# The spread of B into PSUM: its bf16 parts and its selecting columns on 128 partitions instead of 48

## The chip, the cores and the metric

One core of one Trainium2 chip runs the whole program. The metric is the device time of one execution in microseconds. The launch has 3 timed runs of the kernel before.

## What is computed

An image of 128 x 128 tokens with 64 channels goes through two blocks, each a token mixer and a feed-forward part with a residual sum: row attention, a sigmoid recurrence, a selective state-space scan over the 16384 tokens in both directions, and a mixture of 8 experts. The change is in the scan, of which the reference says:

```
dA = jnp.exp(dt[..., None] * A)
dBx = dt[..., None] * Bm[:, :, None, :] * xc[..., None]
def step(h, inp):
    dA_t, dBx_t, C_t = inp
    h = dA_t * h + dBx_t
    y = jnp.einsum('bds,bs->bd', h, C_t)
    return (h, y)
...
y_fwd = _mamba(x_flat, *params)
y_bwd = jnp.flip(_mamba(jnp.flip(x_flat, axis=1), *params), axis=1)
```

There are 128 inner channels (d) and 16 states (s). B (`Bm`) and C hold one number for each token and state, the same for all channels.

## The kernel before

The program is a row of stages, and barriers separate them. The scan is the longest, from about 760 to 2530 us of the span. It works on chunks of 1024 tokens (`TC`), 16 forward (`forward`, chunks 0 to 15) and then 16 backward (`backward`, 16 to 31). In each chunk the channels lie on the 128 partitions and the tokens along the free axis, and the 16 states come one after another. All five engines run the same list of units (chunk n, state s), written out in program order by `run`; semaphores with counts hold them together. Nothing is scheduled by a tool.

For one state s of a chunk:

- ACT makes the decay exp(dt A_s), into an SBUF ring `s_dA` (`decay_v`, L1469) or, for some states, into PSUM (`decay_g`, L1474).
- The input dt B_s x is made in one of three ways. For the states in `BY_VECTOR` (8 of 16 forward, 10 of 16 backward) PE spreads row B_s over 128 partitions into the PSUM tile `s_pu` (`spread_b`, L1303), and DVE multiplies it there by `s_dtx` (L1611). For `BY_SCALAR` (4 forward, none backward) ACT scales transposed data and PE turns them into `s_pu` (L1294). The remaining states (4 forward, 6 backward) have B_s spread by a DMA into `s_bb`, and POOL multiplies (L1546).
- DVE scans: h = decay * h + input (L1635), with two tiles `s_pu` used in turn, so that PE may spread for state s only once the scan of state s-2 is done.
- POOL multiplies h by C_s, which a DMA has spread into `s_cc`, giving `s_hc` (`read_c`, L1553). PE adds it up over the states in `s_py` with an identity as weights (`total`, L1316). A ring of 4 tiles `s_hc` ties POOL to PE: POOL may write the tile of state s once PE has added that of state s-4.

The spread of B_s by PE works on three bf16 parts (high, middle, low) of B in f32. `part_high`, `part_rest` and so on make them one chunk ahead, SP stores them and loads them again as `bcs`, 48 rows = 3 parts x 16 states of 1024 tokens, one half of the tile for each parity of the chunk. The weights are one column of `sel` (48 x 16, ones at rows s, 16+s and 32+s), repeated 128 times, so that the sum of the three parts reaches every output partition. Each half of 512 tokens takes one matmul and one weight load; the whole program has 288 spreads and so 576 of each.

Between these, PE also does the convolution (L1249), the projections of the next chunk and, going backward, the output projection (`project`, L1345, 64-column matmuls).

At the head of the scan SP issues `load_n(0)`, `load_n(1)`, `load_flat(0)` (L1684), `store_parts(0)`, `load_parts(0)` and then the spreads by DMA. POOL sets `s_zero` (L1565) and then waits for its first work, `part_rest` (L1533). The functions that the diff touches are these:

Of the kernel before, what the change touches and what calls it, by code (L numbers as in the profile page):

```python
# [6 lines left out]
BF16 = mybir.dt.bfloat16  # L7
# [942 lines left out]
INNER, STATES, RANK, TAPS = 128, 16, 4, 4  # L950
TC = 1024
# [14 lines left out]
def state_space_stage(nc, c, W, y_scratch, rows, nd, split):  # L966

    with ExitStack() as ctx:
        def sb(name, shape, dt=F32):
# [4 lines left out]
            z=sb("ss_wz", [D, INNER]), bc=sb("ss_wbc", [INNER, BCW]), dt=sb("ss_wdt", [INNER, INNER]),  # L974
            out=sb("ss_wout", [INNER, D]), cb=sb("ss_cb", [INNER, 1]), db=sb("ss_db", [INNER, 1]),
            dd=sb("ss_D", [INNER, 1]), dg=sb("ss_dg", [INNER, INNER]), A=sb("ss_A", [INNER, STATES]),
            sel=sb("ss_sel", [3 * STATES, STATES], BF16))


        zero = sb("ss_zero", [D, PAD + 1])  # L980
# [141 lines left out]
def state_scan(nc, c, nd, k, y_scratch, rows, split):  # L1122
# [9 lines left out]
    with ExitStack() as ctx:  # L1132
# [4 lines left out]
            return c.sem("s_" + name)  # L1137
        ns = sb("n", [128, 2, TC + 2 * PAD])
        xc, dt, dtx = sb("xc", [128, 2, TC]), sb("dt", [128, 2, TC]), sb("dtx", [128, 2, TC])
        bcs = sb("bcs", [3 * STATES, 2, TC], BF16)  # L1140
        brow = sb("brow", [BCW, TC])
        flat, rest = sb("flat", [128, FLAT]), sb("rest", [128, FLAT])
        parts = sb("parts", [128, 3, FLAT], BF16)
# [75 lines left out]
        def _(pe):  # L1219
# [77 lines left out]
            def spread_b(w, n, par, s):  # L1297

                if s == w.v[0]:
                    pe.wait_ge(p_loaded[par], 8 * (n + 2 - par))  # L1300
                need(pe, scanned, n * U + s - 1)
                for hf in halves:
                    ins = nc.tensor.matmul(p_u[s % 2][:, hf],  # L1303
                                           lhsT=k["sel"][:, s:s + 1].to_broadcast([3 * STATES, 128]),
                                           rhs=bcs[:, par, hf], start=True, stop=True)
                ins.then_inc(b_made, 1)

# [213 lines left out]
        @block.gpsimd  # L1521
        def _(pool):
            def linear_and_log(w, m, par):

                pool.wait_ge(relu_made, m + 1)
                pool.wait_ge(log_made, m + 1)
                nc.gpsimd.tensor_tensor(tc[:, :], tc[:, :], tb[:, :], ALU.add).then_inc(sum_made, 1)

            def part_rest(w, m, par):
                pool.wait_ge(high, m + 1)  # L1530
                need(pool, lowest, m)
                need(pool, middle, m)
                nc.gpsimd.tensor_tensor(rest[:, :], flat[:, :], parts[:, 0, :], ALU.subtract).then_inc(remained, 1)  # L1533

            def part_low(w, m, par):
                pool.wait_ge(middle, m + 1)
                pool.wait_ge(remained, m + 1)
                nc.gpsimd.tensor_tensor(parts[:, 2, :], rest[:, :], parts[:, 1, :], ALU.subtract).then_inc(lowest, 1)

            def inject(w, n, par, s):  # L1540
                r = w.g.index(s)
                if r == 0:
                    pool.wait_ge(dtx_done, n + 1)
                pool.wait_ge(b_spread[r % B_RING], 16 * (w.upto(G, n, B_RING) + r // B_RING + 1))
                need(pool, scanned, w.past(G, n, s, lambda v: B_RING))
                nc.gpsimd.tensor_tensor(dbx[:, r % B_RING, :], dtx[:, par, :], bb[:, r % B_RING, :],  # L1546
                                        ALU.mult).then_inc(g_injected, 1)

            def read_c(n, s):
                pool.wait_ge(c_spread[s % C_RING], 16 * (n * (U // C_RING) + s // C_RING + 1))  # L1550
                pool.wait_ge(scanned, n * U + s + 1)
                need(pool, summed, n * U + s + 1 - RING)
                nc.gpsimd.tensor_tensor(hc[:, s % RING, :], h[:, s % RING, :], cc[:, s % C_RING, :],  # L1553
                                        ALU.mult).then_inc(read, 1)

            def unit(w, n, par, s, before, nxt):
                mw, m, mpar, ms = after(w, n, par, s + INJECT_AHEAD, nxt)
                if mw is not None and ms in mw.g:
                    inject(mw, m, mpar, ms)
                if s:  # L1560
                    read_c(n, s - 1)
                elif before is not None:
                    read_c(n - 1, U - 1)

            nc.gpsimd.memset(zero[:, :], 0.0).then_inc(zeroed, 1)  # L1565
            prepare = [(8, part_rest), (9, linear_and_log), (10, part_low)]
            assert min(forward.g) >= INJECT_AHEAD
            run(pool, unit, lambda w: prepare)
            read_c(ALL - 1, U - 1)
# [3 lines left out]
        def _(dve):  # L1573
# [64 lines left out]
                if mw is not None and ms in mw.v:  # L1638
                    inject(mw, m, mpar, ms)

            dve.wait_ge(zeroed, 1)
            prepare = [(9, lost), (10, step_sum), (12, dt_x)]
            tail = {forward: (), backward: [(LAG_SUM - 1, gate), (14, add_x)]}
            run(dve, unit, lambda w: prepare, tail.get)
# [4 lines left out]
        @block.sync  # L1649
        def _(sp):  # L1650
            way_of = lambda m: backward if m >= NC else forward

            def load_n(m):
                if m >= 2:
                    sp.wait_ge(conv, m - 1)
                need(sp, z_made, m - NC - 1)
                W_ = TC + 2 * PAD
                for half in range(2):
                    sp.dma_start(ns[half * D:(half + 1) * D, m % 2, :],
                                 nd[:, base(m) + 1 - half:base(m) + 1 - half + W_]).then_inc(n_loaded[m % 2], 16)  # L1660

            def spread_row(dst, m, row, spread):
                src = rows[m // NC][m % NC, row, :].rearrange("(a t) -> a t", a=1).to_broadcast([128, TC])
                sp.dma_start(dst, src).then_inc(spread, 16)

            def spread_c(n, s):
                if s == 0:
                    sp.wait_ge(r_stored, 16 * (n + 1))
                need(sp, read, n * U + s + 1 - C_RING)
                spread_row(cc[:, s % C_RING, :], n, STATES + s, c_spread[s % C_RING])  # L1670

            def spread_b(n, s):
                w = way_of(n)
                r = w.g.index(s)
                if r == 0:
                    sp.wait_ge(r_stored, 16 * (n + 1))
                need(sp, g_injected, w.upto(G, n) + r + 1 - B_RING)
                spread_row(bb[:, r % B_RING, :], n, s, b_spread[r % B_RING])

            def load_flat(m):  # L1680
                sp.wait_ge(r_stored, 16 * (m + 1))
                need(sp, remained, m)
                src = rows[m // NC][m % NC, 0:STATES, :].rearrange("r (b t) -> (r b) t", t=FLAT)
                sp.dma_start(flat[:, :], src).then_inc(f_loaded, 16)  # L1684

            def store_parts(m):
                sp.wait_ge(lowest, m + 1)
                sp.dma_start(split[m // NC][m % NC, :, :, :].rearrange("k s (b t) -> (s b) k t", t=FLAT),
                             parts[:, :, :]).then_inc(p_stored, 16)

            def load_parts(m):
                sp.wait_ge(p_stored, 16 * (m + 1))
                need(sp, b_made, way_of(m).upto(V, m - 1))
                sp.dma_start(bcs[:, m % 2, :],
                             split[m // NC][m % NC, :, :, :].rearrange("k s t -> (k s) t")).then_inc(p_loaded[m % 2], 16)

            def store_y(n):
                sp.wait_ge(y_taken, 2 * n + 2)
                sp.dma_start(y_scratch[:, base(n):base(n) + TC], yo[:, :]).then_inc(y_stored, 16)

            def load_y(n):
                if n == NC:
                    sp.wait_ge(y_stored, 16 * NC)
                need(sp, y_joined, n - NC)
                sp.dma_start(yf[:, :], y_scratch[:, base(n):base(n) + TC]).then_inc(y_loaded, 16)

            load_n(0)
            load_n(1)
            load_flat(0)
            store_parts(0)  # L1710
            load_parts(0)
            for s in range(4):
                if s in forward.g:
                    spread_b(0, s)
            for n in range(ALL):
                last = n == ALL - 1
                for s in range(U):
                    if s == 8 and 0 < n <= NC:
                        store_y(n - 1)
                    if n >= NC and s == (10 if n == NC else 3):  # L1720
                        load_y(n)
                    m, ms = n + (s + 4) // U, (s + 4) % U
                    if m < ALL and ms in way_of(m).g:
                        spread_b(m, ms)
                    spread_c(n, s)
                    if s == 8 and not last:
                        load_flat(n + 1)
                    if s == 13 and not last:
                        store_parts(n + 1)
                    if s == 14 and not last:  # L1730
                        load_parts(n + 1)
                    if s == 11 and n + 2 < ALL:
                        load_n(n + 2)
# [278 lines left out]
```

## Time and profile before

| | |
|---|---|
| median of 3 runs | 2724.7 us (2724.25 to 2729.43) |
| profiled execution, its own time | 2724.38 us |
| its span, first to last instruction | 2722.6 us |
| mean granted TensorE clock | 0.938 |
| PE, DVE, ACT, POOL busy | 2412.6, 2180.0, 1798.4, 1940.2 us |

The span is what the trace covers; the profiled execution's own time is 1.8 us longer. The granted clock is a share of full speed: 1.00 is 2.4 GHz and 0.50 is 1.2 GHz, and a value between them is a stretch that has both. Busy time of an engine counts the time in which its instructions ran. PE's weight loads are listed apart (PEld), since they overlap its matmuls.

### The profile page before, as it was taken

How to read it: one execution, taken by the hardware profiler on the slowest of the kernel's cores; microseconds unless marked ns; L12 is line 12 of the kernel's file. 1: busy time of each engine (PE TensorE's matmuls, PEld its weight loads, DVE VectorE, ACT ScalarE, POOL GpSimd, SP SyncE). 2: the span in 40 equal slices, each digit the busy share in tenths (PEclk: the TensorE clock that was granted, in tenths of full speed). 3: DMA queues.
4: the chain of work that ended last, by engine and by line, in shares of the span. 5: the costliest groups of instructions: out<-in, count | busy, mean ns of one | idle time of the engine just before them, and what ended most of it. 6: DMA issues, size and time to landing. Idle time of an engine off the chain costs nothing. (4 is left out here: it accounts for less than half of the span.)

```text
span 2722.6 us, 40183 instructions
## 1 busy us (share of the span) xinstructions
PE 2412.6 (89%) x10620; PEld 1195.4 (44%) x10620; DVE 2180.0 (80%) x2229; ACT 1798.4 (66%) x4094; POOL 1940.2 (71%) x1197
## 2 busy tenths in 40 slices
PE   6999999857459899999999999999999999998587
PEld 6577667624324334434433433333333333333533
DVE  4455555560639999999999999999999999998766
ACT  4688778743657778878877875665566556653376
POOL 3900000030239999999999999999999999999379
PEclk7799999969679999999999999999999999999799
DMA  3000000000146767676666767777777677775022
GB/s 66 11 10 10 10 8 9 7 1 0 43 130 222 220 227 228 223 230 220 229 228 221 234 226 250 243 237 235 238 247 238 225 235 246 239 223 189 3 62 62
DMA packets 186408, 421.08 MB, mean 155 GB/s; under 512 B 66548, under 2 KB 87513, under 8 KB 186330
## 3 DMA queue, kind: packets, MB, share of 16 engines
q1 hardware_dynamic: 184794, 416.01, 48.1%
q10 hardware_dynamic: 1536, 4.20, 0.5%
q8 instruction: 29, 0.48, 0.1%
q14 instruction: 49, 0.40, 0.0%
HBM read 387.63 MB, written 24.12 MB: 151 GB/s over the span
## 5 line engine op out<-in xcount | busy, mean ns | idle before, releaser
L1553 POOL TENSOR_TENSOR s_hc<-s_h,s_cc 128x1024 f32<-128x1024 f32 x512 | 1201.2, 2364 | 62.9 <-PE s_py L1316 44.5
L1316 PE MATMUL s_py<-s_hc,ident 128*128 128x512 f32 x2048 | 1019.0, 623 | 8.6 <-DVE s_yo L1598 8.6
L1635 DVE TENSOR_TENSOR_SCAN s_h<-s_dA,s_state,s_pu 128x1024 f32<-128x1024 f32 x330 | 770.4, 2342 | 29.5 <-PE s_pu L1294 6.1
L1316 PEld LDWEIGHTS s_py<-s_hc,ident 128*128 128x128 f32 x2048 | 365.1, 194 | 456.1 <-issue 419.3
L1469 ACT ACTIVATE s_dA<-s_dt,ss_A 128x1024 f32<-128x1024 f32 x352 | 401.7, 1142 | 9.1 <-ACT s_brow L1432 7.7
L1474 ACT ACTIVATE s_pu<-s_dt,ss_A 128x1024 f32<-128x1024 f32 x160 | 178.4, 1115 | 319.1 <-DVE s_h L1635 313.9
L1546 POOL TENSOR_TENSOR s_dbx<-s_dtx,s_bb 128x1024 f32<-128x1024 f32 x160 | 378.0, 2363 | 7.4 <-DMA s_bb<-rows_scratch 7.4
L1611 DVE TENSOR_TENSOR s_pu<-s_pu,s_dtx 128x1024 f32<-128x1024 f32 x288 | 349.7, 1214 | 24.5 <-PE s_pu L1303 24.5
L1635 DVE TENSOR_TENSOR_SCAN s_h<-s_pu,s_state,s_dbx 128x1024 f32<-128x1024 f32 x150 | 350.2, 2335 | 16.8 <-ACT s_pu L1474 16.6
L234 POOL MEMSET rn_n_add<- 128x1 f32 x1 | 0.1, 103 | 403.9 <-POOLq L78 403.9
L1303 PE MATMUL s_pu<-s_bcs,ss_sel 48*128 48x512 bf16 x576 | 175.2, 385 | 92.4 <-DVE s_h L1635 92.3
L628 ACT ACTIVATE ar_ex<-ar_sc,ar_mn 128x128 f32<-128x128 f32 x512 | 199.1, 390 | 44.3 <-DVE ar_mn L534 44.2
L530 DVE TENSOR_TENSOR ar_sc<-ar_pss,at_bias 128x512 f32<-128x512 f32 x128 | 88.5, 692 | 109.8 <-PE ar_pss L468 105.7
L1303 PEld LDWEIGHTS s_pu<-s_bcs,ss_sel 48*128 48x128 bf16 x576 | 33.6, 95 | 307.9 <-DVE s_h L1635 198.5
L1452 ACT ACTIVATE s_sT<-s_dtxT,s_bT 128x128 f32<-128x128 f32 x512 | 156.4, 388 | 0.2
L481 PE MATMUL ar_pst<-ident,ar_ex 128*128 128x128 f32 x1024 | 151.0, 292 | 0.7 <-ACT ar_exT L621 0.7
L1902 PE MATMUL ee_ps<-ex_we,ex_xg 128*128 128x512 f32 x256 | 112.7, 601 | 30.2 <-DMA ex_xg<-ex_xT 30.2
L481 PEld LDWEIGHTS ar_pst<-ident,ar_ex 128*128 128x128 f32 x1024 | 126.3, 194 | 16.3 <-ACT ar_ex L628 0.8
L1249 PE MATMUL s_pp<-s_n,ss_taps 128*128 128x512 f32 x256 | 124.4, 611 | 9.9 <-DMA s_n<-n_scratch 9.9
L544 DVE SCALAR_TENSOR_TENSOR ar_og<-ar_gate,ar_pso 128x128 f32<-128x128 f32 x128 | 36.8, 288 | 97.4 <-PE ar_pso L494 97.4
L1920 ACT ACTIVATE ee_hw<-ee_ps,ex_wt 128x64 f32<-128x64 f32 x384 | 91.9, 316 | 14.8 <-PE ee_ps L1902 5.1
L1481 ACT COPY s_state<-s_h 128x1 f32<-128x1 f32 x510 | 86.8, 179 | 18.5 <-DVE s_h L1635 17.9
(267 smaller groups left out, 3700.6 us busy)
## 6 DMA issues: line engine op xcount, KB each, us to landing
s_cc<-rows_scratch SPq DMA_DIRECT2D x512, 512.0 KB, 4.6
s_bb<-rows_scratch SPq DMA_DIRECT2D x160, 512.0 KB, 5.0
s_n<-n_scratch SPq DMA_DIRECT2D x64, 258.0 KB, 5.6
y_scratch<-s_yo SPq DMA_DIRECT2D x16, 512.0 KB, 5.4
s_yf<-y_scratch SPq DMA_DIRECT2D x16, 512.0 KB, 6.4
x_tok<-in_x_dram SPq DMA_DIRECT2D x16, 256.0 KB, 4.5
at_xg<-at_xT SPq DMA_DIRECT2D x64, 64.0 KB, 2.0
n_scratch<-ss_turned SPq DMA_DIRECT2D x32, 128.0 KB, 2.3
```

The lines of the kernel that those rows point to most:

```text
L481: ins = nc.tensor.matmul(ps_t[:, tile(h)], lhsT=ex[:, j % 2, h, :], rhs=c.ident[:, :], start=True, stop=True)
L628: ins = nc.scalar.activation(ex[:, j % 2, h, :], sc[:, j, h, :], ACT.Exp, bias=mn[:, j, h:h + 1], scale=-1.0, accum_out=tot[:, j % 2, h:h ...
L1249: ins = nc.tensor.matmul(p_p[:, hf], lhsT=k["taps"][:, int(w.back), pair, :], rhs=ns[:, par, at:at + HALF], start=(pair == 0), stop=(pair ...
L1303: ins = nc.tensor.matmul(p_u[s % 2][:, hf], lhsT=k["sel"][:, s:s + 1].to_broadcast([3 * STATES, 128]), rhs=bcs[:, par, hf], start=True, st ...
L1316: ins = nc.tensor.matmul(p_y[:, hf], lhsT=c.ident[:, :], rhs=hc[:, s % RING, hf], start=(s == 0), stop=(s == U - 1))
L1452: ins = nc.scalar.activation(sT[:, r % TURN_RING, j, :], dtxT[:, j, :], ACT.Copy, scale=bT[:, par, j, s:s + 1])
L1469: nc.scalar.activation(dA[:, w.d.index(s) % w.decay_ring, :], dt[:, par, :], ACT.Exp, scale=k["A"][:, s:s + 1]).then_inc(v_decayed, 1)
L1474: nc.scalar.activation(p_u[s % 2][:, :], dt[:, par, :], ACT.Exp, scale=k["A"][:, s:s + 1]).then_inc(g_decayed, 1)
L1546: nc.gpsimd.tensor_tensor(dbx[:, r % B_RING, :], dtx[:, par, :], bb[:, r % B_RING, :], ALU.mult).then_inc(g_injected, 1)
L1553: nc.gpsimd.tensor_tensor(hc[:, s % RING, :], h[:, s % RING, :], cc[:, s % C_RING, :], ALU.mult).then_inc(read, 1)
L1611: nc.vector.tensor_tensor(p_u[s % 2][:, :], p_u[s % 2][:, :], dtx[:, par, :], ALU.mult).then_inc(v_injected, 1)
L1635: nc.vector.tensor_tensor_scan(out=flow(h[:, s % RING, :]), data0=flow(decays), data1=flow(inputs), initial=begun, op0=ALU.mult, op1=ALU.a ...
```

## The change

The tile `bcs` and the tile `sel` get all 128 partitions; rows 48 to 127 of both hold zeros. `sel` was already cleared and then filled with ones by three selections, which now run over 128 partitions. `bcs` gets a memset of its own on POOL at the head of the scan, after that of `s_zero`. The DMA that loads the parts still writes 48 rows. The spread's matmul and weight load now name 128 rows. DVE waits for both memsets, and SP waits for both before `load_flat(0)`, since its third DMA writes into the cleared tile.

```diff
-            sel=sb("ss_sel", [3 * STATES, STATES], BF16))
+            sel=sb("ss_sel", [128, STATES], BF16))
...
-        bcs = sb("bcs", [3 * STATES, 2, TC], BF16)
+        bcs = sb("bcs", [128, 2, TC], BF16)
...
                 for hf in halves:
                     ins = nc.tensor.matmul(p_u[s % 2][:, hf],
-                                           lhsT=k["sel"][:, s:s + 1].to_broadcast([3 * STATES, 128]),
+                                           lhsT=k["sel"][:, s:s + 1].to_broadcast([128, 128]),
                                            rhs=bcs[:, par, hf], start=True, stop=True)
...
             nc.gpsimd.memset(zero[:, :], 0.0).then_inc(zeroed, 1)
+            nc.gpsimd.memset(bcs[:, :, :], 0.0).then_inc(zeroed, 1)
...
-            dve.wait_ge(zeroed, 1)
+            dve.wait_ge(zeroed, 2)
...
-                sp.dma_start(bcs[:, m % 2, :],
+                sp.dma_start(bcs[0:3 * STATES, m % 2, :],
...
             load_n(0)
             load_n(1)
+            sp.wait_ge(zeroed, 2)
             load_flat(0)
```

No instruction changes its place. On POOL, one row is new at the head of the scan; `s_bcs` is the tile of the parts, and the row after it is the first work that waits for data:

```order
 L1521 UNCONDITIONAL_BRANCH
 L1565 MEMSET s_zero 128x1
+L1566 MEMSET s_bcs 128x2048
 L1533 TENSOR_TENSOR s_rest<-s_flat,s_parts 128x128
 L1527 TENSOR_TENSOR s_tc<-s_tc,s_tb 128x1024
```

Behind the new memset the row of POOL's work is as it was.

## Rows read from the trace of the kernel before

**Rows 1.** busy time by stretch (start and end us, length, then each engine)

```profile
core 0: us, PE busy (x) PEld busy (x) DVE busy (x) ACT busy (x) POOL busy (x), PEclk, DMA share, GB/s
...
1200.00:1400.00 200.00, 186.22 (x592) 80.85 (x590) 187.84 (x103) 156.85 (x302) 187.47 (x87) 1.00 0.68 225
...
2200.00:2400.00 200.00, 186.72 (x466) 72.51 (x467) 196.19 (x116) 119.17 (x174) 199.06 (x94) 0.97 0.73 237
```

**Rows 2.** who waited for whom, whole scan, 780 to 2480 us

```profile
POOL s_hc L1553 <- PE s_py L1316: 44.5, 59, 2.6
...
DVE s_pu L1611 <- PE s_pu L1303: 24.5, 50, 3.1
```

**Rows 3.** POOL's waits, 1700 to 2520 us

```profile
POOL s_hc L1553 <- PE s_py L1316: 7.0, 16, 2.5
```

**Rows 4.** busy time by stretch, one chunk each, columns as in rows 1

```profile
796.76:850.48 53.72, 46.39 (x140) 20.34 (x138) 49.23 (x27) 44.43 (x87) 47.41 (x23) 0.91 0.66 224
...
1010.36:1063.64 53.28, 49.75 (x158) 21.53 (x157) 49.47 (x28) 41.50 (x80) 49.16 (x24) 1.00 0.68 219
...
1752.03:1806.45 54.42, 51.06 (x129) 19.61 (x129) 53.35 (x31) 31.88 (x46) 54.11 (x26) 0.97 0.75 241
...
1915.18:1969.20 54.02, 49.61 (x130) 19.02 (x129) 53.25 (x31) 32.04 (x46) 53.99 (x26) 1.00 0.72 240
1969.20:2023.56 54.36, 49.52 (x130) 19.05 (x129) 53.40 (x31) 31.87 (x46) 54.36 (x26) 1.00 0.76 241
2023.56:2077.56 54.00, 49.32 (x130) 18.93 (x129) 53.24 (x31) 32.05 (x46) 53.78 (x26) 1.00 0.71 241
2077.56:2133.53 55.97, 52.62 (x126) 21.27 (x124) 53.51 (x32) 31.87 (x46) 53.46 (x25) 0.91 0.73 238
```

**Rows 5.** PE in order of time, two chunks

```profile
1795.49 0.60 PE L1303 MATMUL s_pu<-s_bcs,ss_sel 48*128 48x512 bf16 x2 [2.67 <-DVE s_h L1635]
...
2120.74 1.03 PE L1303 MATMUL s_pu<-s_bcs,ss_sel 48*128 48x512 bf16 x2 [2.67 <-DVE s_h L1635]
```

**Rows 6.** POOL in order of time, 2110 to 2145 us

```profile
2131.77 2.35 POOL L1553 TENSOR_TENSOR s_hc<-s_h,s_cc 128x1024 f32<-128x1024 f32 x1 [2.50 <-PE s_py L1316]
```

**Rows 7.** busy time by short stretch, columns as in rows 1

```profile
792.80:796.20 3.40, 3.40 (x13) 1.68 (x11) 0.78 (x1) 1.82 (x2) 0.00 (x0) 0.50 0.72 263
796.20:799.60 3.40, 3.40 (x4) 1.40 (x5) 3.29 (x3) 3.40 (x8) 2.70 (x2) 0.50 0.98 401
...
1796.30:1799.70 3.40, 3.40 (x7) 1.36 (x6) 3.40 (x3) 0.86 (x1) 3.40 (x3) 0.50 0.81 299
1799.70:1803.10 3.40, 3.40 (x19) 2.20 (x19) 3.30 (x4) 2.75 (x6) 3.40 (x2) 1.00 0.10 25
...
2120.60:2124.00 3.40, 3.26 (x5) 1.30 (x6) 3.40 (x4) 0.00 (x0) 3.40 (x2) 0.50 0.72 224
2124.00:2127.40 3.40, 3.40 (x13) 2.46 (x11) 3.30 (x3) 3.31 (x5) 3.40 (x3) 0.50 0.32 117
```

**Rows 8.** the tile s_bcs, by operation (ns least/median/most, first and last start)

```profile
L1303 PEld LDWEIGHTS s_pu<-s_bcs,ss_sel x576: 91/95/148, 794.3 to 2503.3; 48*128 48x128 bf16 x192
L1303 PE MATMUL s_pu<-s_bcs,ss_sel x576: 373/377/632, 794.3 to 2503.5; 48*128 48x512 bf16 x192
```

**Rows 9.** the tile s_n, by operation, columns as in rows 8

```profile
L1249 PE MATMUL s_pp<-s_n,ss_taps x256: 590/592/1223, 764.0 to 2414.2; 128*128 128x512 f32 x128
...
L1232 PE MATMUL s_pp<-s_n,ss_wz x64: 588/590/694, 1659.3 to 2479.6; 64*128 64x512 f32 x64
```

**Rows 10.** groups by line and shape: POOL's largest memset

```profile
L1824 POOL MEMSET ex_xg<- 64x2048 f32 x1 | 1.8, 1799 | 0.1
```

**Rows 11.** all engines in order of time, start of the scan

```profile
776.35 0.33 SPq L1684 DMA_DIRECT2D s_flat<-rows_scratch  x1
...
778.49 0.43 POOL L1533 TENSOR_TENSOR s_rest<-s_flat,s_parts 128x128 f32<-128x128 f32 x1 [19.93 <-ACT s_parts L1459]
...
794.28 1.89 PE L1303 MATMUL s_pu<-s_bcs,ss_sel 48*128 48x512 bf16 x4
```

## The prediction

> **What bounds the kernel now.** I read the busy time by stretch first. Forward, no engine is full: in 200 us PE is busy 186.2, DVE 187.8 and POOL 187.5 us, at clock 1.00. Backward, POOL is: 199.1 of 200 us, with DVE at 196.2 and PE at 186.7 us, and the granted clock is 0.97 [rows 1]. Then the waits of the whole scan: POOL waits 44.5 us for PE's sums, in 59 waits, and DVE waits 24.5 us for the spread that this change touches, in 50 waits [rows 2]. Of POOL's 44.5 us only 7.0 fall into the backward half, in 16 waits [rows 3]. So backward the end is set by POOL, and anything PE gains there can give back at most those 7.0 us. Forward the three engines take turns, and a faster or slower spread passes partly through.
>
> Next I cut the trace at the first scan of some chunks [rows 4]. Chunk length and clock go together. Backward chunks at clock 1.00 take 54.02, 54.36 and 54.00 us, mean 54.13. A chunk at 0.97 takes 54.42 us; 0.97 of 54.42 us means 2 x 0.03 x 54.42 = 3.3 us at half speed. The chunk at 0.91 takes 55.97 us, with 2 x 0.09 x 55.97 = 10.1 us at half speed. So a short dip of the clock costs about 0.3 us and the long one 1.84 us. The long one is seen on POOL, which there waits 2.50 us for PE's sums [rows 6].
>
> What makes the dips: in each backward chunk PE waits 2.67 us for a scan, and then the spread comes first [rows 5]. The clock falls around that hole. What happens next differs. At 1796.3 us the clock fell just behind the spread (which ran from 1795.49 for 0.60 us); in the 3.4 us after that PE did only full-row work, and the clock was back at 1.00 [rows 5, 7]. At 2120.6 us it fell just ahead of the spread; PE was busy 3.26 of the next 3.40 us, the two spread matmuls among it, and the clock stayed at 0.50 [rows 5, 7]. The same at the head of the scan: from 792.8 to 796.2 us PE was busy all of 3.40 us, 1.89 of them with four spread matmuls (from 794.28), and the clock stayed at 0.50 through the next 3.4 us [rows 7, 11]. So two of two low stretches with spreads in them did not bring the clock back though PE was busy, and the one without did. The spread is the only work in these stretches with 48 rows. That is my reading, on three stretches: a matmul on 48 rows helps the clock less than one on 128.
>
> **The change, part by part**, against the profiled execution's own 2724.4 us (span 2722.6 and 1.8 around it; the median of the three runs, 2724.7, is 0.3 above).
>
> *The memset.* The nearest row is POOL's memset of 2048 f32 elements on each of 64 partitions, 1.8 us [rows 10]; this one has 2048 bf16 elements on 128. I take 1.8; by bytes it would be 0.9. POOL's first work comes at 778.49 us, after 19.93 us without any, so the memset can run from 758.6 to 760.4 us [rows 11]. SP's new wait is over at 760.4, and its `load_flat(0)` goes out only at 776.35 us, held by the stored rows [rows 11]; behind it on SP stand all later loads, which thus move by nothing. Cover: 16 us. DVE's wait ends even further ahead of its first work. Cost 0; without the cover it would be 1.8 us, once.
>
> *The three selections and the memset of `sel`* have the same elements per partition: 0.
>
> *The spread itself.* There are 576 matmuls, median 377 ns, and as many weight loads, median 95 ns [rows 8]. What 128 rows cost is bounded by a pair in f32 with the same 512 columns: 592 ns on 128 rows, 590 on 64 [rows 9]. So between 0 and 2 ns for each matmul. All 576 on the path would be 576 x 2 = 1.2 us; on DVE's 50 waits it is 50 x 4 ns = 0.2 us (two matmuls each). I take +0.1, ends 0 and +1.2.
>
> *The clock.* If rows count, three things change. (a) In a low stretch that holds a spread, the clock comes back one stretch or more sooner. The chunk with the long dip becomes one with a short dip: 54.42 - 55.97 = -1.55 us. (b) The head of the scan: chunk 0 takes 53.72 us at clock 0.91, a like chunk at 1.00 takes 53.28 [rows 4]. Its excess is 0.44 us, of which I take half, -0.2. (c) Some short dips don't happen at all, since the spread behind the hole now counts in full. The hole itself, 2.67 us, stays, and it is longer than the spread's 0.60 us; so I expect most of the dips to remain, and take two fewer, 2 x 0.3 = -0.6 us. Together -2.35 us. The ends: nothing, if rows do not count, and all, if every dip goes. All is POOL's 7.0 us of waits backward and the 0.44 us of chunk 0, -7.4 us.
>
> Forward the clock is 1.00 anyway [rows 1], so DVE's 24.5 us of waits for spreads stay as they are: they come from when PE starts the spread, which is not moved.
>
> Sum: 2724.4 + 0 + 0.1 - 2.35 = 2722.1, say 2722 us.
>
> **The Trainium skill on this.** "TensorE: Matmul & The Clock Gate", in Part 1, "What's actually happening", has the clock set by how busy PE has recently been, and names no rows. By that rule the change gives the clock nothing, since busy time stays the same, and the sum is 2724.5. The trace agrees only in part: PE was busy 3.26 and 3.40 us of 3.40 and the clock did not rise [rows 7]. This is the second rival below.
>
> **Rivals.**
>
> *Most dips go* (0.20). For it: the hole is the same in every chunk, and yet three backward chunks in a row keep 1.00 [rows 4], so a small shift of the work is already enough to spare a chunk its dip. Against it: the hole is several times the spread. Price: -7.4 + 0.1, so 2717.1 us, and somewhat less gain if only the most go: 2719.
>
> *Rows do not count for the clock, or zeros do not* (0.22). The change then does nothing but 0.1 us of longer spreads: 2724.5 us. For it: three stretches are few; in the stretch at 2120.6 PE was idle for 0.14 us, and the next one, 2124.0 to 2127.4, is low as well with PE at 3.40 [rows 7]; the rows that I add hold only zeros, which may count as no work. Against it: the head of the scan, where PE had no idle time at all.
>
> *The hole meets the clock badly* (0.08, slower). The place is the same hole of 2.67 us. Chunks last 54.0 to 54.4 us, and the clock is granted and taken back at moments that do not follow the chunks: three chunks got through, one had the long dip. A long dip costs 1.84 us. An execution in which more chunks have it is slower, and the three runs of before already lie 5.2 us apart. With the chunks shifted by the change and rows not counting, three more long dips make 3 x 1.84 = 5.5 us, which is where it decides the sign: 2730 us. Against it: if rows count, the long dips are just what goes.
>
> **How the numbers follow.** No change that this kernel's measurement can tell is within 0.2% of 2724.7, so 2719.3 to 2730.1 us. The likeliest case, a few microseconds (0.50), gives 2722, with a range of its own from 2719 to 2724.5, so that 0.05 of it counts as faster. With the 0.20 of the first rival that makes 0.25 faster. The 0.08 is slower, and the rest, 0.67, the same. The range goes down to 2716, below the case in which all dips go, and up to 2729, which holds the second rival with the spread of the runs: 2716 to 2729.
>
> **What the profile after would show.** The spread's rows read 128*128 and still 377 ns in the median, at most 2 more (above 387 my third term is wrong). A memset of `s_bcs` at 758.6 us, 0.9 to 1.8 us long, and `load_flat(0)` still about 16 us behind it. No chunk backward with 10 us of low clock; the clock of the backward stretches at 0.97 to 0.99, and above 0.99 if most dips go. POOL's waits for PE backward down from 7.0 to about 4 us. Wherever the clock fell ahead of a spread, it comes back at the first stretch full of work. Backward chunks without a dip still take 54.0 to 54.4 us; were these shorter, POOL would not be the bound there. The prediction is wrong if the low stretches with spreads stay low as before, or if forward chunks, at 1.00 before and after, change their length.

## The result and the profile after

The changed kernel takes 2708.8 us in the median of 9 executions (2705.3 to 2719.9), the kernel before 2724.3 (2721.8 to 2729.4) beside it. The ratio is 0.9948 with a 95% interval of 0.9934 to 0.9962, so the change gains 0.5%, 14 us by the ratio (the two medians lie 15.5 us apart). I had forecast 2722, with 2716 to 2729 as the range: the gain is more than five times what I gave it, and the time lies below the range. The profiled execution of the changed kernel took 2713.7 us, its span is 2712.0. Three executions of 4.1 to 5.9 ms, two of the kernel before and one of the run x_cols below, are in no median and no ratio here.

The page of the changed kernel, busy time of the engines and three of the costliest groups (matmul of the sums, DVE's product in PSUM, the spread):

```profile
PE 2348.0 (87%) x10543; PEld 1232.0 (45%) x10620; DVE 2180.0 (80%) x2229; ACT 1799.2 (66%) x4094; POOL 1941.6 (72%) x1198
...
L1316 PE MATMUL s_py<-s_hc,ident 128*128 128x512 f32 x2048 | 988.8, 608 | 16.5 <-DVE s_yo L1599 16.2
...
L1612 DVE TENSOR_TENSOR s_pu<-s_pu,s_dtx 128x1024 f32<-128x1024 f32 x288 | 349.2, 1213 | 16.5 <-PE s_pu L1303 14.2
...
L1303 PE MATMUL s_pu<-s_bcs,ss_sel 128*128 128x512 bf16 x499 | 162.4, 396 | 123.3 <-DVE s_h L1636 119.2
```

The sums' matmul has a mean of 608 ns here; on the page of before, the same 2048 matmuls had 623. The spread's own did not get shorter: 396 ns in the mean, and a median of 379 against 377 [rows 8]. (77 of its 576 records are missing from this trace.) DVE waits 14.2 us for spreads instead of 24.5 [rows 2].

The scan by its two halves, columns as in [rows 1], cut at the first scan of chunks 0 and 16 and at the end of the last one. First the forward half before, then both halves after:

```profile
796.76:1644.16 847.40, 785.84 (x2458) 340.77 (x2457) 791.87 (x433) 663.11 (x1277) 792.98 (x368) 0.99 0.69 227
```

```profile
793.22:1631.04 837.82, 749.76 (x2419) 354.43 (x2457) 792.08 (x432) 663.22 (x1277) 791.94 (x368) 0.99 0.70 229
1631.04:2499.90 868.86, 780.13 (x1977) 336.45 (x2013) 846.99 (x490) 502.07 (x725) 857.78 (x397) 0.95 0.73 235
```

The forward half takes 837.8 us instead of 847.4, 9.6 less, at the same clock, and the backward half 868.9 instead of 867.8 at a lower one (0.95 for 0.97). PE is busy for less time forward, though its work was not made less. (39 matmul records of this half are missing from this trace; the traces x_again and x_base below have all of them, and show 31 us less.) Of the 10.6 us between the two spans 9.6 are thus the forward half's, 3.5 lie ahead of the scan, and the backward half and what follows it took 1.1 and 1.4 us more. And some chunks of the changed kernel:

```profile
1002.93:1055.72 52.79, 47.58 (x155) 22.36 (x156) 49.51 (x27) 41.52 (x80) 49.08 (x24) 1.00 0.70 222
...
1792.63:1846.69 54.06, 46.79 (x126) 19.98 (x128) 53.19 (x32) 31.95 (x46) 53.91 (x26) 1.00 0.75 239
1846.69:1901.09 54.40, 49.32 (x126) 21.45 (x127) 53.28 (x32) 31.85 (x46) 54.02 (x26) 0.94 0.73 240
```

The forward chunk at 1002.93 us is chunk 4, the one that [rows 4] show before with 53.28 us: 52.79 now, 0.49 less, both at 1.00. This chunk takes 53.28 to 53.30 us in all four traces with 48 or 64 rows in the spread, and 52.78 to 52.85 in all seven with 80 or more (the runs are below). The backward chunks look as before, 54.06 us without a dip and 54.40 with 6.5 us of low clock (2 x 0.06 x 54.4), against 54.02 to 54.36 without in [rows 4].

Where the forward half got its time is seen in the waits of that half, first before and then after:

```profile
POOL s_hc L1553 <- PE s_py L1316: 37.5, 43, 2.6
...
DVE s_pu L1611 <- PE s_pu L1303: 19.9, 45, 1.6
...
DVE s_h L1635 <- PE s_pu L1294: 7.8, 13, 1.6
```

```profile
POOL s_hc L1553 <- PE s_py L1316: 33.2, 37, 1.4
...
DVE s_pu L1612 <- PE s_pu L1303: 11.2, 32, 3.0
...
DVE s_h L1636 <- PE s_pu L1294: 4.7, 6, 0.8
```

DVE's waits for PE fall from 27.7 to 15.9 us, 11.8 less, and POOL's from 37.5 to 33.2.

What changed on PE is best seen at a spread that stands between full-row matmuls without a wait. PE in order of time in the changed kernel (two matmuls of L1325, two of the spread, four sums):

```profile
1243.83 1.02 PE L1325 MATMUL s_py<-s_xc,ss_dg 128*128 128x512 f32 x2
1244.69 0.59 PE L1303 MATMUL s_pu<-s_bcs,ss_sel 128*128 128x512 bf16 x2
1245.12 1.88 PE L1316 MATMUL s_py<-s_hc,ident 128*128 128x512 f32 x4
```

From the start of the first row to the end of the third it is 1245.12 + 1.88 - 1243.83 = 3.17 us. In the kernel before, at the same place of another chunk, it is 1201.97 + 1.98 - 1200.49 = 3.46 us:

```profile
1200.49 1.02 PE L1325 MATMUL s_py<-s_xc,ss_dg 128*128 128x512 f32 x2
1201.44 0.60 PE L1303 MATMUL s_pu<-s_bcs,ss_sel 48*128 48x512 bf16 x2
1201.97 1.98 PE L1316 MATMUL s_py<-s_hc,ident 128*128 128x512 f32 x4
```

Both matmuls of L1325 take the same, and then the spread starts 0.95 us after them instead of 0.86, the sums start 0.53 us after the spread instead of 0.43, and the four sums take 1.98 us instead of 1.88. Each of the three is 0.10 us, in a different place: one on the way into the 48 rows and two on the way out, 0.30 us in all. It is so wherever a spread stands among full-row matmuls without a wait: from the last full matmul to the spread the starts lie 525 ns apart in the median of 116 places before, and 429 in 60 after; from the second spread matmul to the first sum 306 and 216, and from there to the second sum 533 and 429. The weight loads tell why. In the kernel before, and then in the changed one, around a spread and the sums behind it:

```profile
1201.44 0.11 PEld L1303 LDWEIGHTS s_pu<-s_bcs,ss_sel 48*128 48x128 bf16 x2 [0.76 <-issue]
1201.97 0.30 PEld L1316 LDWEIGHTS s_py<-s_hc,ident 128*128 128x128 f32 x2 [0.42 <-issue]
```

```profile
1191.19 0.10 PEld L1303 LDWEIGHTS s_pu<-s_bcs,ss_sel 128*128 128x128 bf16 x1 [0.24 <-issue]
1191.62 0.10 PEld L1303 LDWEIGHTS s_pu<-s_bcs,ss_sel 128*128 128x128 bf16 x1 [0.33 <-issue]
1191.83 0.41 PEld L1316 LDWEIGHTS s_py<-s_hc,ident 128*128 128x128 f32 x2
```

Before, the first weight load of the sums starts at 1201.97 us, 0.42 us after the spread's loads were over, and just as the sums' first matmul does. After, each load starts as soon as the matmul ahead of it has begun: at 1191.83 us, while the second spread matmul runs. So in these traces the load for a spread on 48 rows, and the first full load behind it, is not taken ahead of the running matmul. That the next matmul waits for it is my reading of these starts. I call this a seam: the extra time at a change of height, the number of rows that a matmul names. None of its time shows as PE idle or as a longer spread; it is in the start of the next instruction and in the duration of the one behind it.

### The profile page after: what moved, and what is told of

Its sections match the earlier page's. It is cut to its first block and busy times, and to the rows that moved or that the text cites. A ratio compares the mean times of both kernels' runs of the same rounds, so it can differ in the third digit from the quotient of the medians.

```text
span 2712.0 us, 40108 instructions
## 1 busy us (share of the span) xinstructions
PE 2348.0 (87%) x10543; PEld 1232.0 (45%) x10620; DVE 2180.0 (80%) x2229; ACT 1799.2 (66%) x4094; POOL 1941.6 (72%) x1198
## 5 line engine op out<-in xcount | busy, mean ns | idle before, releaser
L1316 PE MATMUL s_py<-s_hc,ident 128*128 128x512 f32 x2048 | 988.8, 608 | 16.5 <-DVE s_yo L1599 16.2
L1316 PEld LDWEIGHTS s_py<-s_hc,ident 128*128 128x128 f32 x2048 | 388.8, 194 | 386.6 <-issue 314.2
L1612 DVE TENSOR_TENSOR s_pu<-s_pu,s_dtx 128x1024 f32<-128x1024 f32 x288 | 349.2, 1213 | 16.5 <-PE s_pu L1303 14.2
L1303 PE MATMUL s_pu<-s_bcs,ss_sel 128*128 128x512 bf16 x499 | 162.4, 396 | 123.3 <-DVE s_h L1636 119.2
L1303 PEld LDWEIGHTS s_pu<-s_bcs,ss_sel 128*128 128x128 bf16 x576 | 43.3, 99 | 312.3 <-DVE s_h L1636 205.9
```

The lines of the kernel that those rows point to most:

```text
L1303: ins = nc.tensor.matmul(p_u[s % 2][:, hf], lhsT=k["sel"][:, s:s + 1].to_broadcast([128, 128]), rhs=bcs[:, par, hf], start=True, stop=True)
L1316: ins = nc.tensor.matmul(p_y[:, hf], lhsT=c.ident[:, :], rhs=hc[:, s % RING, hf], start=(s == 0), stop=(s == U - 1))
L1612: nc.vector.tensor_tensor(p_u[s % 2][:, :], p_u[s % 2][:, :], dtx[:, par, :], ALU.mult).then_inc(v_injected, 1)
```

## The experiments

All kernels are the changed one with an edit, unless it says otherwise. The length of the forward half is a sharp measure, since the clock hardly dips there. Where a run below gives its two halves, the rows are busy times by stretch with columns as in [rows 1], cut at the first scan of chunks 0 and 16 and at the end of the last scan.

**x48: 128-row tiles, but a spread on 48 rows.**

```diff
-lhsT=k["sel"][:, s:s + 1].to_broadcast([128, 128]),
-rhs=bcs[:, par, hf], start=True, stop=True)
+lhsT=k["sel"][0:48, s:s + 1].to_broadcast([48, 128]),
+rhs=bcs[0:48, par, hf], start=True, stop=True)
```

> The changed kernel, but the spread's matmul and weight load name rows 0 to 47 again; the 128-row tiles, both memsets and the waits stay. Theory S (seams): the time of before comes back, 2724 us, since what the change took away is PE's extra time where the number of rows changes: 525 instead of 429 ns from the start of a full-row matmul to the start of the spread, and 306 + 533 instead of 216 + 429 ns from the second spread matmul over the first sum to the second sum, together 0.3 us per spread. Rival M (the gain lies in the head of the scan or in where things come to lie, not in the matmul's rows): 2709 to 2713 us as with the change. Forward chunks of 1 second parity: S 53.3 and 52.3 us, M 52.8 and 51.9.

Measured: 2724.8 us, ratio to before 0.9994 (0.9969 to 1.0018). The gain is gone with the memsets and waits still in place.

```profile
793.56:1640.85 847.29, 787.42 (x2458) 340.78 (x2457) 791.91 (x432) 663.52 (x1277) 792.67 (x368) 0.99 0.68 227
1640.85:2509.45 868.60, 810.67 (x2015) 315.40 (x2014) 847.52 (x490) 502.46 (x725) 859.80 (x397) 0.96 0.71 236
```

The place shown above takes 1251.91 + 1.98 - 1250.42 = 3.47 us here, and the forward half 847.29 us, that of before. So it is the rows of the matmul, and nothing at the head of the scan.

**x64: 64 rows** (the same lines with 64).

> The changed kernel with 64 rows in the spread (48 in use, 16 zero). Theory S with the array's rows taken in sizes of 32, 64 and 128: the seams stay, 525 and 306 ns, and the time is that of before, 2724 us. Rival C (what counts is how many rows work, through the granted clock): 16 of the 80 added rows bring a fifth of the 15 us, so 2721 us. Rival: any size other than 48 avoids the seam, 2709 us.

Measured: 2721.4 us, ratio 0.9992 (0.9974 to 1.0010), forward half 847.34 us. PE at the place shown above, and the halves:

```profile
1248.26 1.02 PE L1325 MATMUL s_py<-s_xc,ss_dg 128*128 128x512 f32 x2
1249.22 0.60 PE L1303 MATMUL s_pu<-s_bcs,ss_sel 64*128 64x512 bf16 x2
1249.75 1.98 PE L1316 MATMUL s_py<-s_hc,ident 128*128 128x512 f32 x4
```

```profile
791.44:1638.78 847.34, 786.05 (x2458) 340.50 (x2457) 791.91 (x433) 663.46 (x1277) 792.54 (x368) 0.99 0.68 226
1638.78:2506.95 868.17, 803.71 (x2015) 310.53 (x2014) 847.34 (x490) 502.32 (x725) 859.82 (x397) 0.97 0.72 236
```

1249.75 + 1.98 - 1248.26 = 3.47 us, as with 48. Sixteen more rows bring nothing in the forward half; the rival "any size but 48" falls. The whole time is what rival C expected, 2721 us; more on this with x80.

**x80: 80 rows** (the same lines with 80).

> The changed kernel with 80 rows in the spread (48 in use, 32 zero). Theory S with sizes of 32, 64 and 128: 80 rows need the full size, no seam, 429 and 216 ns, and the time is that of the change, 2709 us. Rival C (rows in proportion, through the clock): two fifths of the gain, 2718 us. If a seam stands wherever two matmuls name different numbers of rows, 2724 us.

Measured: 2718.0 us, ratio 0.9960 (0.9939 to 0.9980), forward half 839.3 us.

```profile
1247.73 1.02 PE L1325 MATMUL s_py<-s_xc,ss_dg 128*128 128x512 f32 x2
1248.59 0.60 PE L1303 MATMUL s_pu<-s_bcs,ss_sel 80*128 80x512 bf16 x2
1249.02 1.88 PE L1316 MATMUL s_py<-s_hc,ident 128*128 128x512 f32 x4
```

```profile
796.54:1635.88 839.34, 755.74 (x2457) 354.49 (x2456) 792.16 (x432) 663.24 (x1277) 792.35 (x368) 0.99 0.68 229
1635.88:2506.37 870.49, 788.03 (x2014) 338.81 (x2013) 847.28 (x490) 502.15 (x725) 857.93 (x397) 0.94 0.70 235
```

1249.02 + 1.88 - 1247.73 = 3.17 us, as with 128. Between 64 and 80 rows the whole seam disappears, though 80 and 128 are different numbers of rows. So what counts is not the number of rows as such. By the whole times alone rival C, a gain in proportion to the rows, would stand: it expected 2721 and 2718 us, and 2721.4 and 2718.0 were measured. The forward half speaks against it, with nothing of the 9.6 us at 64 rows and 8.1 of them at 80. In the profiled execution the backward half, 870.5 us at clock 0.94, is what makes the whole slower than with 128 rows, with 102 us of low clock in it against 44 in x_again. The ten executions of x80 had a median clock of 0.936, the nine of the change 0.941. Why the clock was lower there, by the 80 rows or by chance, is not shown.

**x_ones: ones instead of zeros in the unused rows** (`memset(bcs[:, :, :], 1.0)`; their weights are zero).

> The changed kernel with its memset of the parts' tile to 1.0 instead of 0.0: rows 48 to 127 of the moving operand hold ones, the weights there stay zero, so the sums are the same. If zeros count as no work for the clock, low stretches backward get fewer here and the time falls by up to 5 us below the change; theory S and the reading that rows count whatever they hold expect the time of the change, 2709 us, and the same granted clock within 0.01.

Measured: 2711.7 us, ratio 0.9948 (0.9927 to 0.9969), the ratio of the change. Its profiled execution was quick, 2697.5 us, but mostly since the stages ahead of the scan took 781.4 us in it. The backward clock was 0.97. That is no more than in executions with zeros (0.97 in x_again, with 44 us of low clock backward in both), so nothing speaks for zeros counting less.

**x_quart and x_alt: four matmuls of 256 columns per spread**, all on 128 rows in the first, on 48, 128, 48 and 128 rows in the second.

```diff
-for hf in halves:
+for q, r in enumerate((48, 128, 48, 128)):
+    at = slice(q * 256, q * 256 + 256)
     ins = nc.tensor.matmul(p_u[s % 2][:, at],
+        lhsT=k["sel"][0:r, s:s + 1].to_broadcast([r, 128]),
+        rhs=bcs[0:r, par, at], start=True, stop=True)
```

> The changed kernel with each spread cut into four matmuls of 256 columns, all on 128 rows, with four weight loads instead of two: the control for the next run. Theory S (seams between row sizes) sees none here: forward chunks of 1024 tokens at full clock take 52.8 and 51.9 us as with the change, at most 0.2 us more for the smaller pieces (four weight loads of 99 ns, each beside a matmul that streams 107 ns).

> The same four matmuls of 256 columns with 48, 128, 48 and 128 rows: no more work than in the control, but twice the changes of size of the kernel before (four for each spread instead of two). Theory S: two changes made even forward chunks 53.29 instead of 52.80 us, so four make them 53.8 us or more, since DVE also waits for the two that now lie inside the spread; the whole 10 us or more above the kernel before's 2724. Rival (what costs is any 48-row matmul, as such): half of the spread's work is on 48 rows, so half of the loss, 53.05 us and 2717 us.

Measured, one execution each: 2715.0 us and 2757.4 us. First the control, then the alternating one, at the same place:

```profile
1249.35 1.02 PE L1326 MATMUL s_py<-s_xc,ss_dg 128*128 128x512 f32 x2
1250.21 0.60 PE L1304 MATMUL s_pu<-s_bcs,ss_sel 128*128 128x256 bf16 x4
1250.65 1.88 PE L1317 MATMUL s_py<-s_hc,ident 128*128 128x512 f32 x4
```

```profile
798.33:1636.55 838.22, 754.56 (x2713) 369.36 (x2712) 791.91 (x432) 663.12 (x1277) 792.31 (x368) 0.99 0.70 229
1636.55:2502.80 866.25, 778.97 (x2330) 352.11 (x2329) 846.72 (x490) 501.86 (x725) 859.48 (x397) 0.96 0.72 236
```

```profile
1206.84 1.02 PE L1326 MATMUL s_py<-s_xc,ss_dg 128*128 128x512 f32 x2
1207.79 0.92 PE L1304 MATMUL s_pu<-s_bcs,ss_sel 48*128 48x256 bf16 x4
1208.55 1.88 PE L1317 MATMUL s_py<-s_hc,ident 128*128 128x512 f32 x4
```

```profile
799.51:1653.69 854.18, 800.89 (x2714) 364.65 (x2713) 791.04 (x432) 663.15 (x1277) 791.57 (x368) 0.99 0.68 224
1653.69:2544.88 891.19, 837.99 (x2331) 347.69 (x2330) 850.46 (x490) 502.35 (x725) 860.71 (x397) 0.95 0.70 230
```

The control takes 1250.65 + 1.88 - 1249.35 = 3.18 us and has a forward half of 838.2 us: smaller pieces cost nothing. With two visits to 48 rows the spread starts 0.95 us after L1325, as before the change, and then lasts 0.92 us instead of 0.60, with three seams inside. The forward half is 854.2 us, 16.0 above the control, where one visit per spread (x48) is 9.1 above it. Chunk 4 takes 53.8 us, where I had expected 53.8 or more by seams and 53.05 by the rival that half of the 48-row work costs half. That rival is out: the cost went up with the changes of size, not with the work on 48 rows. The backward half got longer by 25 us, and the whole by more than I expected. The waits of the backward half, first of the control and then of the alternating one, show where:

```profile
POOL s_hc L1554 <- PE s_py L1317: 4.8, 11, 0.6
```

```profile
POOL s_hc L1554 <- PE s_py L1317: 29.0, 43, 2.8
```

POOL, which bounds this half, waits 24 us longer for PE's sums.

**x_cols: the projection to B and C (L1268) with 128 weight columns instead of 32**, and **x_cols_z: the same and the gate (L1232) on 128 rows instead of 64**, with zeros added to both weight tiles by memsets ahead of the scan.

```diff
-nc.tensor.matmul(p_p[0:BCW, hf], lhsT=k["bc"][:, :], rhs=xc[:, par, hf], ...)
+nc.tensor.matmul(p_p[:, hf], lhsT=k["bc"][:, :], rhs=xc[:, par, hf], ...)
...
-rhs=ns[0:D, par, PAD + hf.start:PAD + hf.stop], ...)
+rhs=ns[:, par, PAD + hf.start:PAD + hf.stop], ...)
```

> The changed kernel with the projection to B, C (L1268, 128 rows but 32 output columns) widened to 128 columns of weights, 96 of them zero. Its seams in the changed kernel's trace are 523, 453 and 525 ns where full matmuls have 429, so 0.21 us for each of two per chunk, and about 0.1 more for the next weight load. If a change in the number of columns is such a seam too, all become 429 ns and forward chunks get 0.1 to 0.3 us shorter, 2 to 4 us in all (2706 us against 2709); if the excess belongs to the matmul itself, nothing moves.

> The same, and the gate's matmul backward (L1232, 64 rows) on 128 rows with zeros as weights beyond 64. It takes away the last seams between row sizes in the scan, two changes in each backward chunk. Backward POOL is busy 198 of 200 us, so theory S expects PE to gain 0.3 us for each chunk there and the time to gain nothing over the run above: 2706 us. If backward PE still sets the pace in places (POOL's waits for it are about 0.5 us in a chunk), up to 3 us more.

Measured: 2710.0 us in the median of nine, ratio 0.9950 (0.9930 to 0.9969), and 2704.0 us in that of five, ratio 0.9934 (0.9913 to 0.9955). In the trace of x_cols the seams around the projection are gone where it follows full matmuls without a wait. But its forward half is 838.22 us, that of the control, and the 2 to 4 us that I had expected did not come. At the projections of chunk 4 one sees why. The first comes after PE has been idle, and from its start to that of the spread behind it are 0.96 us instead of 0.98; behind the second PE waits for ACT in both kernels, 0.84 us instead of 0.69. These seams lie where PE has time. The intervals of both overlap that of the change, so I can't call either a gain over it; x_cols_z has the lowest median of all that I ran, with halves of 838.4 and 862.2 us.

**x_again and x_base: the changed kernel and the kernel before once more, unaltered, for a second trace.**

> The changed kernel once more, unaltered, for a second trace. In its first one the clock was low for 89 us in the backward scan, against 58 us before the change. If that is what 128 rows do to the clock, it is near 89 us again and the backward half takes 869 us; if it only differs from one execution to the next, it can lie anywhere from 44 to 102 us (what six other kernels showed), and the backward half is 0.15 us shorter for each us less. The forward half is 838 us in either case.

> The kernel before once more, unaltered, for a second trace. The forward half is 847.4 us again within 0.5 us, since it has no dips to speak of; the backward half 867 to 870 us. If the low clock backward is a trait of the kernel it is near 58 us; the time up to the scan (796.8 us) goes with the low clock up to there, 0.5 us for each us, whatever the kernel.

Measured: 2709.4 us and 2711.8 us, one execution each; a further one of the kernel before, beside them, took 2727.2. The two traced ones are 2.5 us apart, and yet the forward half shows the whole effect, 837.0 against 847.4 us, where I had expected 838 and 847.4:

```profile
794.27:1631.25 836.98, 753.58 (x2458) 353.62 (x2457) 791.99 (x433) 663.17 (x1277) 791.64 (x368) 1.00 0.70 229
1631.25:2495.75 864.50, 767.66 (x2014) 324.74 (x2013) 845.10 (x490) 501.47 (x725) 857.59 (x396) 0.97 0.72 237
```

```profile
781.41:1628.84 847.43, 784.54 (x2458) 340.02 (x2457) 791.85 (x432) 663.89 (x1277) 792.97 (x368) 0.99 0.69 227
1628.84:2497.88 869.04, 797.50 (x2015) 307.58 (x2014) 847.37 (x490) 502.51 (x725) 859.62 (x397) 0.98 0.72 235
```

PE is busy 753.6 instead of 784.5 us, 31 less. The 128 forward spreads with 0.30 us each would be 38 us, but not every one stands among full-row matmuls without a wait. The low clock backward was 44 us in x_again and 38 in x_base, where the first traces had 89 and 58, so it differs from one execution to the next of the same kernel. The backward half of the changed kernel was 4.4 us shorter with 44 us less of it, 0.10 us for each and not the 0.15 of my expectation; that of the kernel before was not shorter, 869.0 against 867.8 us. x_base came to its scan at 781.4 us, the changed kernel at 794.3. That is no effect of the change: four traces with 48 or 64 rows came to it at 781.4 to 796.8 us, seven with 80 or more at 781.4 to 798.3. My expectation ties it to the low clock up to there. Eleven of the twelve traces lie within 2 us of such a line, from 174 us of low clock and 781.4 to 216 and 799.5; x_again, with 186 and 794.3, lies some 8 us above it, so the low clock is not all. A single execution of this program says little about 14 us; its forward half does.

## Why the prediction was wrong

**What bounds the kernel** was read rightly: forward no engine is full and a gain of PE's passes partly through. By its halves the change gained 9.6 us forward and, where the clock is alike, some 4 backward, of up to 86 us of PE's (288 spreads with 0.30 us each, 3.17 against 3.47).

**The step that failed is "The spread itself"**, the term of +0.1 us with ends of 0 and +1.2. I priced it by the durations of spreads and weight loads [rows 8], compared two shapes by their duration [rows 9], and excluded a gain. The durations were right (median 379 after, 377 before) and do not hold the cost. The cost of 48 rows stood in the starts around them, 0.30 us per spread. With it fell the sentence that DVE's waits forward "stay as they are: they come from when PE starts the spread, which is not moved". The instruction is not moved, but its start is: DVE's waits for spreads went from 19.9 to 11.2 us in the forward half. The chunks show it too: my sign of being wrong, that forward chunks at 1.00 change their length, came up with 53.28 and 52.79 us. The trace of before held all this for a reader who compared starts, 0.95 and 0.53 us at 1200.49 us.

**The clock, -2.35 us**, is not what brought the gain. Mean clocks backward with 48 or 64 rows were 0.98 (x_base), 0.96 (x48) and 0.97 (x64); with 80 or more, 0.95, 0.97, 0.94, 0.97, 0.96, 0.97 and 0.97 (the changed kernel, x_again, x80, x_ones, x_quart, x_cols, x_cols_z). In low time this is 38 to 65 us in the four traces with 48 or 64 rows, and 44 to 102 in the seven with more. More rows did not leave less of it. I had forecast a backward clock of 0.97 to 0.99 and POOL's waits for PE at about 4 us; the changed kernel's first trace has 0.95 and 9.3 us, x_again 0.97 and 5.0. Nor does a spread on 128 rows always end a dip. In the changed kernel the clock fell at 2052.6 us, the spread ran from 2053.40 us, and then:

```profile
2053.40 1.03 PE L1303 MATMUL s_pu<-s_bcs,ss_sel 128*128 128x512 bf16 x2 [3.18 <-DVE s_h L1636]
```

```profile
2052.60:2056.00 3.40, 2.60 (x5) 1.20 (x6) 3.40 (x3) 0.00 (x0) 3.40 (x3) 0.50 0.69 216
2056.00:2059.40 3.40, 3.40 (x12) 2.37 (x11) 3.30 (x3) 2.65 (x5) 3.40 (x2) 0.50 0.45 158
```

PE was busy 2.60 and then 3.40 of 3.40 us, and the clock stayed at 0.50 through both, as in the stretches that I had laid to the 48 rows [rows 7]. PE was idle for the first 0.8 us here, so this stretch and those of [rows 7] are not quite alike. Whether rows count at all for the clock is not settled; forward, where most of the gain is, they brought none through it.

**(a) The long dip** was priced rightly: the chunk with 10.2 us of low clock took 56.04 us in x_base too. With 80 rows or more no backward chunk but the last of the scan has so long a dip, and the longest chunks of these seven traces take 54.5 to 55.1 us; with 48 or 64 rows those of the four take 55.8 to 56.0. So this loss went, but not because dips did: ten of the changed kernel's backward chunks have a dip of 6.8 us in its first trace, and in x48 and x64 it is behind dips of 6.8 us, too, that the longest chunks stand. Whether the rows' weight for the clock has a part in it, or only the shorter work of PE behind the hole, is not shown. **(b) Chunk 0** got 1.6 us shorter, from 53.72 to 52.11 us, and not 0.2. It takes 52.10 us in x_again as well, and 53.78 in x_alt, though that had less low clock in it than the changed kernel (5.9 us against 6.8). So the seams made most of it. **(c) The short dips** were overpriced: in x_again ten backward chunks with 3.4 us of low clock take 54.05 to 54.46 us, nine of them at most 54.20, and the four between them without any take 54.06 to 54.27, where I had 0.3 us for each dip.

The backward half as a whole took 862.2 to 864.5 us at full height and a clock of 0.97, and with seams 867.8 (the first trace of before) to 869.0 us at any clock between 0.96 and 0.98. With 80 or more rows it took 866.3 to 870.5 us with 75 to 102 us of low clock. So backward the change gains about 4 us where the clock is alike, and loses them where it is low for longer. I had held 7.0 us to be the most that could be gained backward [rows 3], which stands. Forward 9.6 and backward about 4 make 13.6 us, near the measured 14; how much backward a single execution gets is left to its clock.

**The memset** was as forecast: 1.80 us, 16 us ahead of the load that now waits for it.

```profile
755.22 1.80 POOL L1566 MEMSET s_bcs<- 128x2048 bf16 x1
...
773.17 0.34 SPq L1685 DMA_DIRECT2D s_flat<-rows_scratch  x1
```

**The rivals.** "Most dips go" was nearest in time (2717.1) but not the cause. "Rows do not count for the clock, 2724.5" may have been right about the clock, and was wrong about the time, since it had the same 0.1 us for the spread. "The hole meets the clock badly" had nothing of the gain; the dips did differ from one execution to the next, as it says. The Trainium skill's rule on the clock ("TensorE: Matmul & The Clock Gate", Part 1, "What's actually happening"), by how busy PE has recently been, leaves the clock without a part in the gain. The trace agrees only in part: PE was busy for 3.40 of 3.40 us at a clock of 0.50 after the change too.

The same page says in Part 2, "LDWEIGHTS (loading the stationary operand)", that 32 rows of weights load in the time of 128. The loads agree: 95 ns on 48 rows, 98 on 128. In Part 3, "The mechanism", it has loads pulled ahead of running matmuls when they go to another row group or to the background weight buffer, and then says that the two overlap only when their row groups differ. By this last sentence the measurement differs: loads of the same height overlap in the changed kernel (the one at 1191.83 us above), and it is the load at a seam that does not.

## What to carry to other kernels

Price a matmul by the time from its start to the start of the next one, in its place between its neighbours, and not by its duration. Where a short matmul of up to 64 rows stands among matmuls of full height, filling its rows with zeros cost 2 ns of duration here and took up to 0.30 us off at each spread; it is worth doing where another engine waits for that matmul, and worth nothing where PE has slack, as the projection to B and C showed. When single executions differ by more than the change, find a stretch without dips of the clock and measure that.

## What the hardware showed beyond this

- The seam has steps: 48 and 64 rows have it against 128, and 80 rows do not. 32 rows were not tried.
- It is 0.10 us on the way to the lower height and 0.20 us on the way back, when the full matmuls have 512 columns in f32 and the clock is 1.00.
- The number of weight columns makes a seam too: 32 beside 128 columns (L1268), in the changed kernel 523, 453 and 525 ns from start to start where full width has 429. In x_cols it is 429 ns where the projection follows full matmuls without a wait.
- A seam in the middle of a spread costs as much as at its edge: 212 to 216 ns from start to start in x_alt, where the same 256 columns take 109 in x_quart.
